# First attention of a fused two-layer kernel: scores formed a second time transposed, the row maximum carried as two rows of the operand stacks, the low parts split between VectorE and GpSimd

## The reference, cut to what matters

```python
B, N, C = x.shape            # 4, 512, 512
q = q.reshape(B, N, H, Dh)   # H = 16 heads of Dh = 32
k = k.reshape(B, M, H, Dh)   # M = 512
v = v.reshape(B, M, H, Dh)
attn = jax.nn.softmax(jnp.einsum('bnhd,bmhd->bhnm', q, k) * scale, axis=-1)
o = jnp.einsum('bhnm,bmhd->bnhd', attn, v).reshape(B, N, C)
```

## Time and profile before

| what | value |
|---|---|
| median of three runs | 3154.22 us |
| the profiled execution | 3148.71 us |
| its span | 3147.0 us |
| busy over the span: PE, DVE, ACT, POOL | 93%, 74%, 66%, 44% |
| granted TensorE clock, mean | 0.976 of full |
| first scores of the stage to the last multiply of `normalise` | 166.0 to 541 us |
| DVE, PE, ACT, POOL busy in these 375 us | 348.2, 331.4, 323.4, 38.0 us |

### The profile page before, as it was taken

One profiled execution on the slowest core, in us unless ns is written; L12 is line 12 of the kernel. 1 busy time (PEld: TensorE's weight loads), 2 busy tenths in 40 slices (PEclk: granted clock), 3 DMA queues, 4 the chain that ended last, 5 costly groups with the idle time before them and its releaser, 6 DMA issues. The chain is left out here.

```text
span 3147.0 us, 56456 instructions
## 1 busy us (share of the span) xinstructions
PE 2921.9 (93%) x15414; PEld 2362.3 (75%) x15414; DVE 2334.2 (74%) x4699; ACT 2086.0 (66%) x4262; POOL 1395.0 (44%) x1761
## 2 busy tenths in 40 slices
PE   6878998887999989999999899999999999899888
PEld 5656665676888877778888688888888888688654
DVE  6679998854777658767776289999999888734376
ACT  4478987422666546566666588888888888533275
POOL 4412000403001065367686377777777777441132
PEclk9989999898999999999999999999999999999999
DMA  6896664206888686545456532332332232286400
GB/s 209 269 226 167 155 158 108 87 27 223 290 265 285 189 265 220 161 140 172 141 171 185 161 97 70 99 99 73 97 97 80 90 97 72 94 293 194 149 21 34
DMA packets 401824, 474.32 MB, mean 151 GB/s; under 512 B 52276, under 2 KB 267220, under 8 KB 401652
## 3 DMA queue, kind: packets, MB, share of 16 engines
q1 hardware_dynamic: 388692, 419.72, 44.1%
q0 software_dynamic: 12960, 52.61, 4.9%
HBM read 304.30 MB, written 167.92 MB: 150 GB/s over the span
## 5 line engine op out<-in xcount | busy, mean ns | idle before, releaser
L2861 POOL TENSOR_SCALAR h_probs<-h_exp,h_rowsum_inv 128x512 f32<-128x512 f32 x512 | 356.1, 695 | 277.4 <-PE h_pT L2709 260.9
L2789 DVE TENSOR_REDUCE h_neg_max<-h_scores 128x1 f32<-128x512 f32 x512 | 349.1, 682 | 142.9 <-PE h_scores L2701 142.7
L2751 ACT ACTIVATE h_exp<-h_scores,h_neg_max 128x512 f32<-128x512 f32 x512 | 355.1, 694 | 110.3 <-DVE h_neg_max L2789 101.0
L2802 DVE TENSOR_TENSOR h_probsT_lo<-h_pT,h_probsT_hi 128x512 fp32r<-128x512 f32 x512 | 347.9, 680 | 0.0
L2709 PEld LDWEIGHTS h_pT<-ident,h_probs 128*128 128x128 f32 x2048 | 254.5, 140 | 71.2 <-POOL h_probs L2861 2.3
L2709 PE MATMUL h_pT<-ident,h_probs 128*128 128x128 f32 x2048 | 307.0, 272 | 0.9 <-POOL h_probs L2861 0.8
L2760 ACT CAST h_probsT_hi<-h_pT 128x512 fp32r<-128x512 f32 x512 | 300.8, 587 | 0.9 <-PE h_pT L2709 0.9
L2977 PE MATMUL k_acc<-k_w_hi,k_cat 128*128 128x512 f32 x512 | 200.6, 392 | 12.4 <-POOL k_w_lo L3058 11.5
L2724 PE MATMUL h_pO<-h_probsT_hi,n_lo 128*128 128x512 f32 x512 | 203.3, 397 | 0.0
L2978 PE MATMUL k_acc<-k_w_lo,k_cat 128*128 128x512 f32 x512 | 200.1, 391 | 0.0
L910 ACT ACTIVATE b_probs<-b_scores,b_neg_max 128x512 f32<-128x512 f32 x256 | 179.8, 702 | 24.8 <-DVE b_neg_max L937 24.8
(11 more groups left out here) (460 smaller groups left out, 9042.5 us busy)
## 6 DMA issues: line engine op xcount, KB each, us to landing
e_w_raw<-in_w SPq DMA_DIRECT2D x24, 1792.0 KB, 7.9
lnT<-g_out SPq DMA_DIRECT2D x160, 256.0 KB, 2.3
n_raw<-lnT SPq DMA_DIRECT2D x64, 512.0 KB, 5.4
e_w_raw<-in_w SPq DMA_DIRECT2D x24, 896.0 KB, 9.9
n_raw<-lnT SPq DMA_DIRECT2D x64, 256.0 KB, 5.3
n_raw<-v SPq DMA_DIRECT2D x64, 256.0 KB, 5.7
cat<-h_cat SPq DMA_DIRECT2D x128, 128.0 KB, 1.8
k_cat<-cat SPq DMA_DIRECT2D x128, 128.0 KB, 4.8
```

What stands on the lines that cost most here:

```text
L2751: nc.scalar.activation(Pr[:, r % 4], pS[r % 2][:], ACT.Exp, bias=nmax[:, r % 4:r % 4 + 1], accum_out=rsum[:, r % 4:r % 4 + 1]).then_inc(ex ...
L2789: v.tensor_reduce(nmax[:, r % 4:r % 4 + 1], pS[r % 2][:], axis=AX, op=ALU.max, negate=True).then_inc(nmax_done.sem, 1)
L2802: v.tensor_tensor(PTl[:, br * HPG + h, :, bass.ts(q, P)], pT[r % 4][:], PTh[:, br * HPG + h, :, bass.ts(q, P)], ALU.subtract).then_inc(lo_ ...
L2861: nc.gpsimd.tensor_scalar(Pn[:, r % 4], Pr[:, r % 4], rinv[:, r % 4:r % 4 + 1], 1.0, ALU.mult, ALU.mult).then_inc(norm_done.sem, 1)
```

## The change

An item becomes a whole head. PSUM holds half a head's scores (2 tiles of 512) in one buffer `scores`, two buffers of half a head's transposed scores, and a bank shared by `pMR` and `pR`. Per head:

- TensorE forms 4 scores tiles in two halves from stacks that now have three parts (96 rows: the product of the two low parts goes); VectorE takes the maxima of a half, 128 x 1024, in one instruction.
- GpSimd (`max_columns`) writes high and low part of minus the maxima as columns 96 and 97 of a zeroed tile `Mx`; TensorE (`max_rows`) turns it by four products with the identity; ScalarE (`max_copy`) copies two rows into rows 96 and 97 of `Qs`; `Ks` has ones there.
- TensorE forms the scores again, transposed (`scores_t`, 98 rows deep), with the maximum already subtracted; ScalarE's exp is the transposed probability: the transposes through PSUM go. The row sum comes from a column of ones in `V` (65 columns per head, heads no longer share `pO`).
- The high part of the first half is VectorE's (`high_a`), of the second ScalarE's (`high_b`). The low part of the first half is GpSimd's (`low_a`, 128 x 1024); of the second VectorE's (`low_b`, 128 x 1024), but in every second head GpSimd takes half of it (`low_c`, 128 x 512). All these read both operands from SBUF.
- `o_copy`, the turning back and `normalise` run once per head.
- The zeros of `rows` go through SyncE's queue, 4 DMAs per group, each a quarter as long. The weight splits become single steps on GpSimd beside even heads (8 to 38), the folds beside 40 and 42, the constants' and first weights' DMAs beside head 4.

```diff
-                for w, stack, parts in ((0, Qs, (0, 0, 1, 1)), (1, Ks, (0, 1, 0, 1))):
+                for w, stack, parts in ((0, Qs, (0, 0, 1)), (1, Ks, (0, 1, 0))):
...
-                wait(sp, s_done.sem, s_done.depth + (n - 1) * UN)
+                wait(sp, st_done.sem, (st_done.depth + (n - 1) * HG0) * HALF)
...
+                for h in range(HG0):
+                    sp.dma_start(rows[bass.ds((n * HG0 + h) * ZR * D, ZR * D)]..., Z[:]).then_inc(z_out, 16)
+            pipeline(sp, NG, 2, [(load, 0), (clear_rows, 1), (store, 2)])
...
+            def max_columns(i, r):
+                pool.wait_ge(nmax_done.sem, nmax_done.done(n))
+                pool.wait_ge(mrow_mm.sem, mrow_mm.free(n))
+                nc.gpsimd.tensor_copy(Mx[:, r % 2, :, STACK], nmax[:, r % 2]).then_inc(mx_hi.sem, 1)
+                pool.wait_ge(mx_hi.sem, mx_hi.done(n))
+                nc.gpsimd.tensor_tensor(Mx[:, r % 2, :, STACK + 1], nmax[:, r % 2], Mx[:, r % 2, :, STACK],
+                                        ALU.subtract).then_inc(mx_done.sem, 1)
+            def low_a(i, r):
+                pool.wait_ge(hi_a.sem, hi_a.done(n))
+                nc.gpsimd.tensor_tensor(PTl[:, h, 0:HALF], Pr[:, r % 2, 0:HALF], PTh[:, h, 0:HALF],
+                                        ALU.subtract).then_inc(lo_a.sem, 1)
+            def low_c(i, r):
+                if third(r):
+                    pool.wait_ge(hi_b.sem, hi_b.done(n))
+                    nc.gpsimd.tensor_tensor(PTl[:, h, HALF], Pr[:, r % 2, HALF], PTh[:, h, HALF],
+                                            ALU.subtract).then_inc(lo_c.sem, 1)
+                if isinstance(n, int):
+                    beside(n)
+            pipeline(pool, NH, ROUND_TRIP, [(max_columns, 1), (low_a, 2), (low_c, 2)], NH)
...
+            pipeline(pe, NH, ROUND_TRIP, [(part(scores, 0), 0), (part(values, 0), 3), (part(values, 1), 3), (max_rows, 1),
+                                          (part(scores, 1), 0), (part(values, 2), 3), (part(scores_t, 0), 1),
+                                          (part(values, 3), 3), (o_rows, 4), (part(scores_t, 1), 1)])
...
+            def exps(i, r, half):
+                act.wait_ge(st_done.sem, st_done.part(n, half))
...
+                nc.scalar.activation(Pr[:, r % 2, half * HALF:(half + 1) * HALF], pST[half][:], ACT.Exp).then_inc(exp_done.sem, 1)
+            def high_b(i, r):
+                nc.scalar.copy(PTh[:, h, HALF:], Pr[:, r % 2, HALF:]).then_inc(hi_b.sem, 1)
+            pipeline(act, NH, ROUND_TRIP, [(high_b, 2), (max_copy, 1), (lambda i, r: exps(i, r, 0), 1), (o_copy, 3),
+                                           (lambda i, r: exps(i, r, 1), 1)])
...
+            def maxima(i, r, half):
+                dve.wait_ge(s_done.sem, s_done.part(n, half))
+                nc.vector.tensor_reduce(nmax[:, r % 2, half * HALF:(half + 1) * HALF], pS[:], axis=AX, op=ALU.max,
                                         negate=True).then_inc(nmax_done.sem, 1)
+            def high_a(i, r):
+                dve.wait_ge(exp_done.sem, exp_done.part(n, 0))
+                nc.vector.tensor_copy(PTh[:, h, 0:HALF], Pr[:, r % 2, 0:HALF]).then_inc(hi_a.sem, 1)
+            def low_b(i, r):
+                dve.wait_ge(hi_b.sem, hi_b.done(n))
+                k = HALF + 1 if third(r) else HALF
+                nc.vector.tensor_tensor(PTl[:, h, k:], Pr[:, r % 2, k:], PTh[:, h, k:], ALU.subtract).then_inc(lo_b.sem, 1)
+            def normalise(i, r):
+                dve.wait_ge(oTr_done.sem, oTr_done.done(n))
+                nc.vector.reciprocal(rinv[:, r % 2], pR[:, :, 2 * DH0]).then_inc(rinv_done.sem, 1)
+                out = O[:, gb, :, h * DH0:(h + 1) * DH0]
+                nc.vector.tensor_reduce(out, pR[:, :, 0:2 * DH0].rearrange("p k (w c) -> p k c w", w=2),
+                                        axis=AX, op=ALU.add).then_inc(osum_done.sem, 1)
+                nc.vector.tensor_tensor(out, out,
+                                        rinv[:, r % 2].unsqueeze(2).to_broadcast([P, QT, DH0]), ALU.mult).then_inc(o_done.sem, 1)
+            pipeline(dve, NH, ROUND_TRIP, [(high_a, 2), (lambda i, r: maxima(i, r, 0), 0), (low_b, 2),
+                                           (lambda i, r: maxima(i, r, 1), 0), (normalise, 4)])
```

More of the change, by code:

```diff
@@ L845, in _, with scores @@
+            pipeline(pool, NH, ROUND_TRIP, [(max_columns, 1), (low_a, 2), (low_c, 2)], NH)
             pool.wait_ge(folded, 2)
-            pool.wait_ge(z_out, 16 * NG)
         @block.tensor
         def _(pe):
-            def scores(i, r):
-                n = i * 2 * UN + r
-                gb, h, q = place(r)
+            def scores(i, r, half):
+                n, gb, h = head(i, r)
                 first = isinstance(i, int) and i == 0 and gb == 0
[L854 to L865, removed]
-                for k in range(QT):
[L867 to L885, removed]
@@ L899, in _ @@
-            pipeline(pe, N, 2 * UN, [(transposes, 3), (scores, 0), (values, 9), (o_transposes, 10)])
+                if half == 0:
+                    if r == 0 and first:
+                        pe.wait_ge(qk_first, QK_LOADS * 16)
+                    if r == (1 if first else gb * HG0):
+                        pe.wait_ge(qk_in[gb], i * QK_LOADS * 16 + QK_LOADS * 16)
+                    pe.wait_ge(nmax_done.sem, nmax_done.part(n - 1, 1))
+                else:
+                    pe.wait_ge(nmax_done.sem, nmax_done.part(n, 0))
@@ new lines, in scores, with max_rows @@
+                for j in range(HALF):
+                    last = nc.tensor.matmul(pS[:, j], Qs[0:STACK, gb, h, bass.ts(half * HALF + j, P)], Ks[0:STACK, gb, h],
+                                            start=True, stop=True)
+                last.then_inc(s_done.sem, 1)
+            def max_rows(i, r):
+                n, gb, h = head(i, r)
+                if isinstance(n, int) and n == 0:
+                    pe.wait_ge(prepared, 3)
+                pe.wait_ge(mx_done.sem, mx_done.done(n))
+                pe.wait_ge(o_done.sem, o_done.past(n, 4))
+                for q in range(QT):
+                    last = nc.tensor.matmul(pMR[0:DEEP, bass.ts(q, P)], Mx[:, r % 2, q], ident_r[:], start=True, stop=True)
+                last.then_inc(mrow_mm.sem, 1)
@@ new lines, in scores_t @@
+            def scores_t(i, r, half):
+                n, gb, h = head(i, r)
+                if half == 0:
+                    pe.wait_ge(mrow_done.sem, mrow_done.done(n))
+                pe.wait_ge(exp_done.sem, exp_done.part(n - 1, half))
+                for j in range(HALF):
+                    last = nc.tensor.matmul(pST[half][:, j], Ks[0:DEEP, gb, h, bass.ts(half * HALF + j, P)],
+                                            Qs[0:DEEP, gb, h], start=True, stop=True)
+                last.then_inc(st_done.sem, 1)
@@ new lines, in values @@
+            def values(i, r, k):
+                n, gb, h = head(i, r)
+                if k == 0:
+                    pe.wait_ge(lo_a.sem, lo_a.done(n))
+                    pe.wait_ge(oT_done.sem, oT_done.past(n, 1))
+                    if h == 0:
+                        pe.wait_ge(v_in[gb], (i + 1) * 16 * HG0)
+                if k == HALF:
+                    pe.wait_ge(lo_b.sem, lo_b.done(n))
+                    if third(r):
+                        pe.wait_ge(lo_c.sem, lo_c.done(i * HG0 + r // 2))
+                nc.tensor.matmul(pO[0:OW], V[:, gb, k, h], PTh[:, h, k], start=(k == 0), stop=False)
+                last = nc.tensor.matmul(pO[0:OW], V[:, gb, k, h], PTl[:, h, k], start=False, stop=(k == QT - 1))
+                if k == QT - 1:
+                    last.then_inc(o_mm.sem, 1)
@@ L927, in o_copy @@
-                nc.scalar.copy(Os[:, pair_buffer(r)], pO[:]).then_inc(oT_done.sem, 1)
-            pipeline(act, N, 2 * UN, [(high, 3), (exps, 1), (o_copy, 9)])
+                act.wait_ge(oTr_done.sem, oTr_done.free(n))
+                nc.scalar.copy(Os[0:OW, r % 2], pO[0:OW]).then_inc(oT_done.sem, 1)
+            pipeline(act, NH, ROUND_TRIP, [(high_b, 2), (max_copy, 1), (lambda i, r: exps(i, r, 0), 1), (o_copy, 3),
+                                           (lambda i, r: exps(i, r, 1), 1)])
@@ L967, in _ @@
-            pipeline(dve, N, 2 * UN, [(low, 4), (maxima, 0), (normalise, 10)])
+            def maxima(i, r, half):
+                n, gb, h = head(i, r)
+                dve.wait_ge(s_done.sem, s_done.part(n, half))
+                if half == 0:
+                    dve.wait_ge(mx_done.sem, mx_done.free(n))
+                nc.vector.tensor_reduce(nmax[:, r % 2, half * HALF:(half + 1) * HALF], pS[:], axis=AX, op=ALU.max,
+                                        negate=True).then_inc(nmax_done.sem, 1)
```

232 lines of the change are left out of this document (114 added, 118 removed).

## The result

The changed kernel takes **3170.6 us** (median of 9 runs, 3163.6 to 3179.7) against 3154.2 of before (9 runs, 3151.1 to 3162.6): ratio 1.0051, 95% interval 1.0038 to 1.0064. It is slower by 16 us; 3170 was forecast. The profiled run, one of the nine, took 3173.7 us, its span is 3172.0.

A forecast was written before the change was run, and what follows sets the result against it. DVE sets the pace, held up by POOL's SBUF reads: 61 steps of 5.82 us plus fill, 8 extras and drain end the stage at 557.4 against 541, +16, so 3170 us. Range 3128 to 3220.

The forecast's parts named there:

- DVE sets the pace, held up by POOL: Attention stage: DVE's own work is 4.7 us per head, but low_b stands 1.3 us while POOL's low_a reads SBUF.
- The step: Time from head to head in the attention stage: 6.08 us even, 5.56 odd, mean 5.82 against 5.68 before.
- A waiting `low_b` goes ahead of POOL's `low_c`: Odd heads: DVE's low_b, waiting since 1.82, runs before the low_c issued at 3.15, giving a 5.56 us step.
- the even step: Even heads, low_b of 1024 columns ending 1.08 after POOL's low_a: next head at 6.08 us.
- a memset at 566.58: Trace of before: POOL's memset went ahead of a waiting DVE instruction; set aside because memsets read nothing.
- The rival with POOL first: Odd heads: low_b waits for low_c also, 39 us, plus some 10 beside splits: 3219 us; chance 0.20.
- DVE is not held up: Rival: low parts meet less often, a 5.3 us chain bounds the head: 3134 us; chance 0.27.
- PE and ACT: Attention stage, per head: PE needs 5.0 us and ACT's chain 5.1, both below the step, adding nothing.
- POOL's other steps: Weight subtracts and DMA issues beside heads: 8 us, from 3 (subtracts), 3 (head 4's issues), 2 (later issues); between 0 and 15.
- Fill: Stage start: first scores at 164.5, head 0 4.2 us, stall for other stacks 4.3, two steps 4.3 + 5.5.
- DMA stayed hidden: Stack loads: six issues and landing take 13.3 us, released 17.5 us ahead of need, so hidden.
- Drain: Stage end, from last maxima to the end: 12.3 us, less 0.7 already in the last step.

The follow-up runs named there:

- pool_writes_only: Changed kernel with GpSimd's low_a and low_c replaced by memsets of about the same time, so it writes but does not read: 3129.7 us, ratio 0.9923 to before.
- order_no_third: Changed kernel without low_c, VectorE's order first maxima, high_a, low_b, second maxima, normalise: 3173.7 us, ratio 1.0061 to before.
- low_a_beside_maxima: Changed kernel without low_c, normalise's multiply in PSUM, VectorE's order maxima, low_b, high_a, maxima, normalise, TensorE's values 2 and 3 first: 3208.6 us, ratio 1.0178 to before.

## Why the prediction was right

- **DVE sets the pace, held up by POOL.** Right, and shown from both sides: without POOL's reads 41 us vanish, and 165 us of reads beside PSUM operands hold neither the subtract nor the maxima (6 us more than before in all).
- **The step.** Forecast 6.08 and 5.56, mean 5.82; measured 6.08 and 5.53, mean 5.81. `low_b` 2.45 and 1.82 in the mean against the 2.4 and 1.9 named. PE idled 54.6 us before the scores, 0.85 per head, where 0.8 was named.
- **A waiting `low_b` goes ahead of POOL's `low_c`.** Right in all 61 heads where it waited, and without `low_c` nearly all heads had the even step. The prediction set a memset at 566.58 aside because it reads nothing; as said above, memsets did go ahead of that DVE instruction and seem to have held it, so the choice was right here, but by a reason that the rows do not bear out. The rival with POOL first (3219) would have needed 512-column `low_b`s of over 3 us.
- **"DVE is not held up" (3134).** Its time is about what the kernel would take if the mechanism were absent (3130 in pool_writes_only); its condition, that the low parts seldom meet, is refuted: they meet in 63 of 64 heads.
- **PE and ACT.** Below the step, as said. `max_rows` was set too high at 0.8: four short products take 0.48 (406.81, L922). It touched nothing here.
- **POOL's other steps.** 8 us forecast, and by the differences of the spacings from 6.07 and 5.53 there are 8.1 us more than the bare steps; but only 5.5 of them are POOL's. The DMA issues of head 4 cost 3.8 (head 5 takes 9.30 instead of 5.53), the later DMA issues 0.5 in each of two odd heads, and the four subtracts of 896 columns 0.2 each; 3, 2 and 3 us in all were forecast for the three. All sixteen weight steps take 1 us longer than in the kernel before (L829 3.1 instead of 2.1), because `low_b` holds them too, which the forecast had not priced. The other 2.7 us are a term that it did not have: in each of the heads 9, 17, 25, 33, 41 and 49 some 0.45, most of it a pause of 0.34 to 0.40 on DVE ahead of the next `high_a`. Each engine's list of steps runs in a loop of eight heads (`ROUND_TRIP`), and this is where DVE's loop begins its next turn. The profile puts four of the six pauses down to no other engine ("issue"):

```profile
476.44 0.69 DVE L1015 CAST b_probsT_hi<-b_probsT 128x1024 fp32r<-128x1024 f32 x1 [0.34 <-issue]
```

- **Fill.** First scores 164.5 forecast, 164.95 measured; stall of the second head 4.3 against 3.7; last maxima end at 545.4 against 557.4 - 12.3 + 0.7 = 545.8. DMA stayed hidden behind that: PE waited for stacks only in these first two places.
- **Drain.** The term that was most mis-sized: 12.3 us (less 0.7) forecast, 15.7 measured (545.4 to 561.1), so the stage ended 19.8 later and not 16. (The parts named in the prediction add up to 12.0, not 12.3.) The way to the last high part took 7.2 instead of 6.2. The low parts took 3.3 instead of 2.6: the working had them at their own time, but there too `low_b` stands for `low_a` and `low_c` for `low_b`. The last values took 1.9 instead of 1.1: TensorE's clock is 0.83 over the drain and 0.56 in its last 6 us, where values start 0.43 apart instead of 0.23. From the copy to the last multiply it took 3.1 instead of 2.1, of which PE's turning back (L958 at 559.47) waited 1.07 for the multiply of the head before (L1035).

```profile
552.61 2.13 DVE L1021 TENSOR_TENSOR b_probsT_lo<-b_probsT,b_probsT_hi 128x512 fp32r<-128x512 f32 x1 [0.86 <-ACT b_probsT_hi L990]
...
554.15 1.73 POOL L888 TENSOR_TENSOR b_probsT_lo<-b_probsT,b_probsT_hi 128x512 fp32r<-128x512 f32 x1
...
556.02 0.66 PE L948 MATMUL b_pO<-b_probsT_hi,b_v 128*65 128x512 f32 x1 [0.62 <-POOL b_probsT_lo L888]
```

That the number was met to 1 us is partly luck. The forecast took before's profiled run as 5.5 us below its median and let the changed kernel lie as far; its profiled run lay 3.2 above. So the two profiled runs differ by 25 us, 19.8 of them in the stage, and the medians by 16. That the 8 us came out is luck as well, since the loop turns made up for what POOL's steps did not cost. What was tested is the step.

What the experiments showed wrong was in their own forecasts: four of nine were missed, by 23 to 71 us, three of them because I summed DVE's time and took the cost of POOL's steps as fixed, when their place in POOL's queue decided.

## What to carry to other kernels

Before work is moved to GpSimd, list for each DVE instruction beside it where its operands lie. Here those that read PSUM ran free, and those that read two operands from SBUF stood still for GpSimd's reads. So did the one-input copy in its fast form, and in one place of the trace that kind seems to have stood still for memsets too. Put GpSimd's reads beside DVE's PSUM readers by the order of work. Then look at what stands behind the small instruction that feeds another engine: a subtract of 1.3 to 2.1 us queued ahead of `max_columns` cost 3 to 5 us through TensorE, and most of it came back by moving it behind (0.5 to 1.4 are left).

## What the runs showed of the hardware that was not expected

- The standing still goes both ways and reaches tiny instructions: `max_columns`' operations of 4 elements take 0.65 and 1.07 us instead of 0.2 beside DVE's SBUF work in order_no_third, 1.18 beside `low_b` in low_a_beside_maxima.
- POOL's memsets beside a DVE subtract cost it nothing (1.224 us in the mean of 32 with 1024 columns), but the one-input L1248 beside memsets takes 1.19 instead of 0.49.
- fp32r products with 128 moving columns: four in 0.48 us, against 0.41 for the four transposes of L958.
